# Layer 0's 4x4 Sinkhorn normalisation of batch 0: one part of eight tiles instead of two parts of four

## The reference

```python
def step(carry, _):
    u, v = carry
    u = -jax.nn.logsumexp(Z + v[..., None, :], axis=-1)
    v = -jax.nn.logsumexp(Z + u[..., :, None], axis=-2)
    return ((u, v), None)
(u, v), _ = jax.lax.scan(step, (u0, v0), None, length=50)
H_res = jnp.exp(Z + u[..., :, None] + v[..., None, :])
...
H_res = (1.0 - g) * I + g * H_res
x_mixed = jnp.einsum('btij,btjc->btic', H_res, x_streams)
```

## Time and profile before

| | us |
|---|---|
| median of 3 runs | 2416.65 (2415.68 to 2420.78) |
| the profiled execution | 2415.36 |
| its span, first to last instruction | 2413.3 |
| of it, the stage `layer0_mix` | 90.5 to 264 |

### The profile page before, as it was taken

How to read it: one execution, slowest core, us unless ns; L and a number is a source line. 1 busy time by engine, 2 the same in 40 slices (tenths; PEclk the granted TensorE clock), 3 DMA queues, 4 the chain that set the end, 5 groups by cost and what they waited for, 6 DMA issues and landing times. The chain is left out here.

```text
span 2413.3 us, 34772 instructions
## 1 busy us (share of the span) xinstructions
PE 2244.0 (93%) x11194; PEld 1817.2 (75%) x11194; DVE 1545.9 (64%) x3821; ACT 1085.7 (45%) x2327; POOL 1016.4 (42%) x1126
## 2 busy tenths in 40 slices
PE   5588897999999999999998896999999999999998
PEld 4454476888888888878777674888888888888886
DVE  4588654777677777766655464657575656666665
ACT  3356433545454544444444231545454545444444
POOL 2543511636354444585845010616252534434341
PEclk9899998999999999999999997999999999999999
DMA  9500356010101010102010464010101010101010
GB/s 348 193 1 10 134 211 222 26 46 25 61 9 61 9 61 11 59 20 66 20 50 6 169 247 144 19 53 17 52 26 54 15 61 9 61 9 61 23 35 31
DMA packets 74020, 164.97 MB, mean 68 GB/s; under 512 B 4704, under 2 KB 38880, under 8 KB 67296
## 3 DMA queue, kind: packets, MB, share of 16 engines
q1 hardware_dynamic: 73504, 162.69, 19.2%
q10 hardware_dynamic: 432, 1.32, 0.2%
HBM read 113.14 MB, written 72.61 MB: 77 GB/s over the span
## 5 line engine op out<-in xcount | busy, mean ns | idle before, releaser
L1632 DVE TENSOR_TENSOR pT<-psum,pT 128x512 fp32r<-128x512 f32 x576 | 386.9, 688 | 258.7 <-ACT pT L1680 256.4
L1532 POOL TENSOR_TENSOR probs_even<-probs_even,rinv 128x1024 f32<-128x1024 f32 (+2 forms) x192 | 240.9, 1255 | 575.6 <-DVE rinv L1623 575.6
L1680 ACT ACTIVATE pT<-psum 128x512 fp32r<-128x512 f32 x576 | 329.2, 596 | 308.8 <-PE psum L1741 308.5
L1618 DVE CUSTOM_DVE_ANT_0 psum<-psum,causal 128x256 f32<-128x256 f32 (+7 forms) x512 | 385.7, 767 | 39.5 <-PE psum L96 35.4
L1671 ACT ACTIVATE probs_even<-psum,nmax 128x1024 f32<-128x1024 f32 (+3 forms) x256 | 204.5, 799 | 252.4 <-DVE nmax L1618 249.0
L1532 POOL TENSOR_TENSOR probs_odd<-probs_odd,rinv 128x896 f32<-128x896 f32 (+2 forms) x192 | 199.4, 1046 | 251.7 <-DVE rinv L1623 251.7
L94 PE MATMUL psum<-keys,q 128*128 128x512 f32 (+3 forms) x768 | 266.3, 347 | 6.8 <-DMA keys<-k_parts 3.1
L96 PE MATMUL psum<-keys,q 128*128 128x512 f32 (+3 forms) x768 | 262.5, 342 | 0.0
L95 PE MATMUL psum<-keys,q 128*128 128x512 f32 (+3 forms) x768 | 262.4, 342 | 0.0
L94 PE MATMUL psum<-pT,vals 128*128 128x512 f32 x576 | 256.3, 445 | 4.1 <-DVE pT L1632 0.2
L1671 ACT ACTIVATE probs_odd<-psum,nmax 128x896 f32<-128x896 f32 (+3 forms) x256 | 176.7, 691 | 148.3 <-DVE nmax L1618 145.6
(11 more groups left out here) (291 smaller groups left out, 4464.2 us busy)
## 6 DMA issues: line engine op xcount, KB each, us to landing
k_parts<-kv_out SPq DMA_DIRECT2D x32, 512.0 KB, 4.5
wq<-wq_copy SPq DMA_DIRECT2D x16, 1024.0 KB, 4.8
wo<-wo_copy SPq DMA_DIRECT2D x16, 1024.0 KB, 4.8
v_parts<-kv_out SPq DMA_DIRECT2D x32, 512.0 KB, 4.0
keys<-k_parts SPq DMA_DIRECT2D x32, 512.0 KB, 4.7
vals<-v_parts SPq DMA_DIRECT2D x64, 256.0 KB, 3.2
acc<-in_x SPq DMA_DIRECT2D x4, 1024.0 KB, 12.2
xn_later<-xn SPq DMA_DIRECT2D x1, 2048.0 KB, 14.3
```

The costliest lines, as they stand in the source:

```text
L1532: pool.tensor_tensor(p, p, rinv[:, u, h:h + 1].to_broadcast([P, (TB - u) * P]), ALU.mult).then_inc(p_ok, 1)
L1618: dve.tensor_tensor_reduce(out=row, in0=row, in1=causal[:, S - n:S], scale=-1.0, scalar=-2 * MASKED, op0=ALU.add, op1=ALU.min, accum_out=n ...
L1632: dve.tensor_tensor(pT[:, n % PT_SLOTS, 1, :], bank[T_BANK + n % 2], f32(pT[:, n % PT_SLOTS, 0, :]), ALU.subtract).then_inc(t_lo, 1)
L1680: act.activation(pT[:, n % PT_SLOTS, 0, :], bank[T_BANK + n % 2], ACT.Copy).then_inc(t_hi, 1)
```

## The change

`PARTS` in `layer0_mix` is 1 instead of 2. The functions and loops follow from it: each half has one multiply on GpSimd, one sum and one reciprocal on VectorE, each over all eight tiles of batch 0 (128x128 elements for the multiply and the sums' input, 128x32 for the factors), with one set of three semaphores. ScalarE's first exponential of `col` (line 574) and VectorE's `memset` (line 522) are one instruction each instead of two. The steps in `between` keep their half numbers.

```diff
         sb = Column(nc, 196, KEPT)
         UQ = 4
         UNITS = NT // UQ
-        PARTS = 2
+        PARTS = 1
```

## The result

| | before | after |
|---|---|---|
| median, 9 runs each | 2416.30 us | 2427.39 us |
| ratio, 95% interval | | 1.0049 (1.0034 to 1.0063) |
| span of the profiled execution | 2413.3 us | 2427.5 us |
| start of half 0 | 93.17 | 96.22 |
| half 0 to the end of half 88 | 118.95 | 130.33 |

The change makes the kernel slower by 11.1 us in the medians, or 0.5% (0.34 to 0.63%, which is 8 to 15 us); 2427.5 was forecast. The spans of the two profiled executions differ by more, 14.2 us: 3.05 of it had come about before half 0, in a stage that the change does not touch, 11.74 lie in the stage itself, and 0.6 were given back after it.

What follows compares the result with a forecast made beforehand. The prediction took the loop of 100 halves, paced by VectorE and GpSimd, as the bound, half 88 setting the stage's end. Its terms summed to +11.5 us, giving 2426.9 (profiled) or 2428.1 (median); forecast 2427.5 us, range 2421.5 to 2432.

Steps and rivals of the forecast that it cites:

- 57 plain halves: Halves not bound by a step, up to half 88: longer sums, reciprocal and multiply add 0.325 us each, +18.5 us.
- 15 maxima: Halves with a maximum, up to half 88: VectorE is the bound and gains 0.19 us each, -2.9 us.
- half 28: Its maximum waited 1.74 us for TensorE; longer plain halves ahead remove the wait, -2.1 us including the maximum's 0.19.
- half 31: Its reciprocal waited 1.22 us for ScalarE; that wait goes, -1.2 + 0.3 = -0.9 us.
- halves 2, 5, 7, 9: Halves with fixed steps, gaining like a maximum: -0.15 us each, -0.6 us.
- halves 41 to 45 and 65 to 69: Addition groups: the projection wait swallows the plain half in front, other additions change -0.05 to -0.14 us; together -0.6 us.
- recentring: Start and recentring: one longer multiply each, less one short instruction, +0.1 us for both.
- rival 4: TensorE falls behind as more idling lowers its clock; small form +3 to +4.5 us, 2431 us; chance 0.12.
- halves 89 and 90: Around the third group's first addition: the wait of 1.55 us balances the longer plain half, no change.
- the cover of the loop's end: Mixing matrices after half 99 were ready some 8.5 us before ScalarE's first scaled stream, hiding the loop's later end.
- That halving the instructions pays: Rival 1: short instructions are mostly fixed cost, plain halves do not grow, step halves gain 7 us, 2409 us; chance 0.04.
- That the loop is not the bound: Rival 3: attention sets half 88 anyway and VectorE only waits less; +3 us at most, 2419 us; chance 0.03.

Runs made afterwards that it cites:

- four_more: Two more rounds (four plain halves) after half 99 of the changed kernel; half 88 ended at 129.54 us, the stage at 183.63 against 181.49.
- unrolled: Kernel before, two parts, with GpSimd's loop over the halves written out; half 88 ended at 119.60 us against 118.95.
- four_tiles: One part of four tiles, tiles 4 to 7 left out of all halves, against the kernel before; half 88 ended at 110.57 us against 118.95.
- recip_four: Changed kernel with the reciprocal taken of four tiles only (16 factors instead of 32); half 88 ended at 122.79 us against 130.33.
- multiply_four: Changed kernel with GpSimd multiplying four tiles only (64 elements instead of 128); half 88 ended at 123.74 us against 130.33.
- one_warm: Changed kernel with 3, 5 and 5 unused TensorE products before the projections of units 0 to 2; ratio to the kernel before 1.0028.
- four_parts: Four parts of two tiles instead of the two parts of the kernel before; half 88 ended at 143.87 us against 118.95.
- two_warm: Kernel before with two unused TensorE products before each projection of units 0 to 2 and nine before unit 0's weighted streams; ratio 1.0011.

## Why the prediction was right

**Half by half.** The sum to the end of half 88 was to be +11.5 us and was +11.38; with the second execution of one part (four_more, whose halves up to 88 are those of after) it was +10.59. Against unrolled, the second execution of two parts, the two are +10.73 and +9.94. So the mechanism and the size are right, but that the sum is met within 0.1 us, and the median by 2427.5 against 2427.39, is luck. By its terms, predicted, after, four_more:

| term | predicted | after | four_more |
|---|---|---|---|
| 57 plain halves | +18.5 | +17.2 | +17.1 |
| 15 maxima | -2.9 | -3.0 | -3.0 |
| half 28 | -2.1 | -2.0 | -2.1 |
| half 31 | -0.9 | -0.6 | -0.9 |
| halves 2, 5, 7, 9 | -0.6 | -0.6 | -0.6 |
| halves 41 to 45 and 65 to 69 | -0.6 | +0.4 | +0.2 |
| recentring | 0.0 | 0.0 | 0.0 |

(The start's longer multiply lies ahead of half 0's sums, which waited 1.10 us instead of 0.99, and so outside this count: +0.11 where I had +0.1 for start and recentring together.)

**Plain halves**: the mechanism is shown by four_tiles, the prices by recip_four and multiply_four. The size was 7% too big: 1.284 instead of 1.32 by columns, mainly because I took 0.39 and 0.43 from layer 1 where the sums here take 0.38 and the reciprocal follows after 0.41, and 416 ns for a multiply that takes 412.

**Halves 28 and 31**: that half 28's wait goes was right, in after and in four_more. Its -2.1 is the 1.74 us of one profile, and with the 2.5 to 3.2 us of the other kernels with two parts the change would have gained about 1 us more there. At half 31 I let the whole wait go, and 0.78 of 1.22 us stayed. The 32 products ahead of half 28's maximum took 6.57 us in after and 5.74 in four_more, where only 0.08 us of wait were left at half 31; that this is the reason is not shown. It is not the change that made them slow: in unrolled they took 6.60.

**Additions**: here a step was wrong. I let the wait for the projection swallow the longer plain half ahead of it, counting TensorE's part as unchanged. It was not: halves 65 and 66 together grew by 0.95 us, since the wait went from 1.19 to 2.03. In one_warm, with the gap filled, the same two halves together took as long as in the kernel before (a difference of 0.00 us), so the swallowing is right and TensorE's part was what failed. It is my rival 4 in its small form; it did not come in the 32 products of the last unit, which took 3.73 us as before. The error was 1.0 us here and 0.6 in the next group (halves 89 and 90 took 0.59 more, where I had said they balance), against 1.3 us too much for plain halves: the errors cancel, and the total is closer than its parts.

**The end**: +11.38 at half 88 became +11.74 at the stage's end, so half 88's delay is the stage's, as said. But the cover of the loop's end was 2.4 us and not 8.5, by four_more; it sufficed, since 3.6 us had been there before and the loop's end moved by 12.94 us, only 1.2 more than the tail. That nothing was lost at the end was right, but the cover was mis-sized by a factor of more than two, and 2.4 us more on the loop's end alone would have used it up.

**Rivals.** That halving the instructions pays is refuted in plain halves (four_tiles, four_parts) and true in halves with a long step, where it was part of the sum. The Trainium skill's page VectorE: DVE Perf Modes, section "The TRN2 errata — SBUF-src ops pay a fixed extra latency per instruction", argued for one large tile; the fixed cost is there in these runs (a reciprocal of 8, 16 and 32 elements took 0.20, 0.25 and 0.35 us), but with two parts it was paid under cover. The one cycle per element at 0.96 GHz of the same section of the Trainium skill makes, as an estimate, 0.017 us for 16 elements, and does not agree with the 0.10 that recip_four took away. That the loop is not the bound is refuted by every run that changed the plain half: the stage followed each of them.

## What to carry to other kernels

When two engines hand work to and fro as here, cut it so that the second part just fills the first part's way through the other engine: a part more costs its instructions, a part less leaves both engines waiting and lengthens each instruction of the chain. Count the chain and each engine's total for every kind of turn; where other work shares an engine, the best number of parts differs from turn to turn, but joining parts in one turn makes that turn wait for all parts of the one before. To say what cover a late result has, follow every consumer down to the end of the stage, also through the order in which a third engine issues its work.

## What the runs showed of the hardware beside this

- A reciprocal on VectorE costs 0.20 us for 8 elements per partition, 0.25 for 16 and 0.35 for 32, some 6 ns per element; sums over 32, 64 and 128 elements 0.13 to 0.21, 0.16 to 0.27 and 0.27 to 0.39 us, some 1 ns per element by rows (0.22 and 0.29 us for 64 and 128, both after a wait).
- GpSimd's multiply with a broadcast factor: 240 ns for 32 elements, 299 ns for 64, 412 ns for 128.
- The same projections of TensorE took 4.33 us with the gap before them filled (granted clock 1.00), 5.40 after 2.1 us of idling in the kernel before and 5.75 after 4.5 us (clock 0.50 at their start). In unrolled 2.1 us of idling cost them no clock.
- Nine products that ended 4.5 us before the next work did nothing for it: its 32 products took 6.48 us in two_warm, and 6.60 in unrolled after 13.34 us of idling.
